# Twelve small layers on one core: later places for four pieces of layer two's keys and values, and a pause of GpSimd in the router

## What is computed

```
x = x + _L0_attn_ref(_layernorm(x), ...)                  # mLSTM and gated MLP
x = x + _L0_ffn_ref(_layernorm(x), wg, shared, experts)   # router, 2 shared and 16 expert blocks
x = x + _L1_xattn_ref(_layernorm(x), ctx_2048, ctx_2048)  # 16 heads, causal, no projections
x = x + _L1_attn_ref(...); x = x + _L1_ffn_ref(...)       # dense attention, quantized linear
x = x + _L2_xattn_ref(_layernorm(x), ctx_2048, mask, wq, bq, wk, bk, wv, bv, wo, bo)  # 16 heads
...
```

## Time and profile before

| | |
|---|---|
| median of three runs | 1213.25 us |
| the profiled execution's own time | 1214.64 us |
| its span, from the first to the last instruction | 1212.8 us |
| TensorE matmuls busy | 1096.0 us, 90% |
| TensorE weight loads busy | 834.8 us, 69% |
| VectorE busy | 655.0 us, 54% |
| ScalarE busy | 548.4 us, 45% |
| GpSimd busy | 223.0 us, 18% |
| the clock that TensorE was granted, mean | 0.954 of full |

### The profile page before, as it was taken

One profiled execution on the slowest core, in us unless ns is written; L12 is line 12 of the kernel. 1 busy time (PEld: TensorE's weight loads), 2 busy tenths in 40 slices (PEclk: granted clock), 3 DMA queues, 4 the chain that ended last, 5 costly groups with the idle time before them and its releaser, 6 DMA issues.

```text
span 1212.8 us, 22806 instructions
## 1 busy us (share of the span) xinstructions
PE 1096.0 (90%) x9168; PEld 834.8 (69%) x9168; DVE 655.0 (54%) x1308; ACT 548.4 (45%) x987; POOL 223.0 (18%) x344
## 2 busy tenths in 40 slices
PE   6888989989999869999787889999999999999885
PEld 2655668865666536777554767788888888887763
DVE  3645252247777267888534644654444445555357
ACT  2132222225666348888553234444444344444365
POOL 4500068002122000000010310011000133222031
PEclk9998999997999889999887899999999999999998
DMA  9611247444663460000200210131111112100000
GB/s 386 264 54 64 82 158 240 156 139 113 181 169 86 162 222 36 2 2 2 113 28 1 87 35 20 35 105 53 36 36 36 52 53 72 60 18 10 1 1 10
DMA packets 38101, 102.46 MB, mean 84 GB/s; under 512 B 4080, under 2 KB 12656, under 8 KB 36336
## 3 DMA queue, kind: packets, MB, share of 16 engines
q1 hardware_dynamic: 33808, 88.91, 22.0%
q0 software_dynamic: 2752, 9.44, 2.5%
q10 hardware_dynamic: 1440, 2.70, 0.6%
HBM read 85.83 MB, written 15.20 MB: 83 GB/s over the span
## 4 chain that ended last, share of the span: by engine, by line
PE 83%; DVE 10%; ACT 3%; issue 2%; DMA 1%; POOL 0%; DVEq 0%; SPq 0%; ACTq 0%; POOLq 0%
PE ps L2161 10%; PE ps L2110 9%; PE ps L433 8%; PE ps L1743 5%; PE ps L1391 5%; PE ps L2144 5%; PE ps L2006 5%; PE ps L2015 4%; PE ps L426 4%; PE ps L488 3%; PE ps L1734 3%; PE ps L1540 3%; PE ps L1076 2%; PE ps L1551 2%; DVE st L1669 2%
## 5 line engine op out<-in xcount | busy, mean ns | idle before, releaser
L2161 PE MATMUL ps<-vv,probT 128*128 128x128 f32 x1024 | 135.3, 275 | 0.2 <-ACT probT L2226 0.2
L2161 PEld LDWEIGHTS ps<-vv,probT 128*128 128x128 f32 x1024 | 124.4, 192 | 0.5 <-ACT probT L2226 0.5
L2226 ACT COPY probT<-ps 128x512 f32<-128x512 f32 (+1 forms) x96 | 45.7, 477 | 121.8 <-PE ps L2144 118.2
L1669 DVE TENSOR_REDUCE st<-ps 128x1 f32<-128x512 f32 x128 | 83.5, 687 | 27.7 <-PE ps L1540 21.5
L2260 ACT ACTIVATE prob<-ps,st,small 128x1024 f32<-128x1024 f32 x64 | 79.9, 1254 | 31.0 <-DVE st L2305 31.0
L2144 PE MATMUL ps<-const,prob 128*128 128x128 f32 x544 | 85.6, 273 | 0.0
L2048 DVE TENSOR_REDUCE small<-vv 128x4 f32<-128x512 f32 x32 | 21.9, 685 | 116.9 <-ACT vv L2031 116.9
L433 PE MATMUL ps<-xT,big 128*128 128x256 f32 x352 | 79.4, 380 | 1.4 <-ACT big L1100 0.7
L1616 ACT ACTIVATE prob<-ps 128x1024 f32<-128x1024 f32 x64 | 65.7, 1029 | 29.0 <-PE ps L1551 27.4
L152 POOL TENSOR_SCALAR small<-small 128x4 f32<-128x4 f32 (+1 forms) x38 | 7.8, 206 | 380.4 <-DVE small L2048 261.1
L2144 PEld LDWEIGHTS ps<-const,prob 128*128 128x128 f32 x544 | 64.2, 141 | 16.7 <-issue 16.4
(11 more groups left out here) (442 smaller groups left out, 2215.5 us busy)
## 6 DMA issues: line engine op xcount, KB each, us to landing
big<-blocks_in SPq DMA_DIRECT2D x22, 768.0 KB, 4.3
big<-ctxT_in SPq DMA_DIRECT2D x32, 512.0 KB, 4.1
key_parts<-w POOLq DMA_DIRECT2D x16, 384.0 KB, 3.4
kt<-key_parts SPq DMA_DIRECT2D x32, 192.0 KB, 3.3
vv<-ctx_in SPq DMA_DIRECT2D x2, 2176.0 KB, 28.7
vv<-early_values SPq DMA_DIRECT2D x4, 1088.0 KB, 12.8
kt<-ctxT_in SPq DMA_DIRECT2D x2, 2048.0 KB, 14.7
kt<-key_parts SPq DMA_DIRECT2D x32, 128.0 KB, 3.1
```

Of the source, the lines that this page charges most:

```text
L1669: dve.tensor_reduce(self.mx[:, u % 2, n:n + 1], k.ps[:, n % 2, :], AX.X, ALU.max).then_inc(s("reduced"), 1)
L2161: last = pe.matmul(k.ps[:, 7, 0:P], k.probT[:, ch * P:ch * P + P], v, start=(ch == 0), stop=(ch == MC))
L2226: copy(k.probT[:, lo:hi], k.ps[:, 5 + t % 2, 0:hi - lo]).then_inc(s(copied), 1)
```

## The change

- `LATE` is 12: pieces 12 to 15 use the second ring, which now lies in `vv` at the columns of batch 1's first half of values. The causal attention reads them, so GpSimd sets the ones column behind that attention's last product (it was done at its start) and counts it on `fsum`; the stores of these pieces wait for it.
- Piece 12 goes from between the router and the experts to behind the causal attention, where 13 was; 13 goes to 14's place, 14 to 15's. Piece 15 goes into the masked attention: its keys behind unit 0's scores, its values behind unit 1's, in banks 4 and 5, and ScalarE copies them ahead of unit 0's exps and ahead of the last queries copy. SyncE stores it, within `reload`.
- GpSimd waits for the fifth `block_h`, the gate of the first expert block, before its last ten split blocks.
- `fsum` is added once piece 15's keys are made (product 31); its readers wait for 2.
- The waits for finished stores at turn 2 on ScalarE and VectorE are taken out.

```diff
-    BANKS = [(4, 5), (0, 1), ... (0, 6), (0, 2), (0, 1), (0, 2), (0, 1), (2, 3)]
-    LATE = 13
+    BANKS = [(4, 5), (0, 1), ... (0, 6), (0, 2), (0, 2), (0, 1), (2, 3), (4, 5)]
+    LATE = 12
...
-        (self.ks, self.vs), (self.late_ks, self.late_vs) = ring(8704), ring(4096)
+        (self.ks, self.vs), (self.late_ks, self.late_vs) = ring(k.big, 8704), ring(k.vv, 2 * MC * VH)
...
     def store(self, queue, n):
+        if n >= self.LATE:
+            queue.wait_ge(self.k.s("fsum"), 1)
...
     def reload(self, sp):
         for b, pieces in enumerate((self.LATE, self.PIECES)):
+            if b:
+                self.store(sp, self.PIECES - 1)
             self.stored(sp, pieces)
...
 # Causal.gpsimd
-        o.step(pool.memset(early.late_vs[:, :, :, 16:17], 1.0))
...
 # Masked.tensor
             if t < 32:
                 scores(t)
+            if t == 0:
+                pe.wait_ge(*self.at("turned_sb", 1))
+                self.early.tensor_keys(pe, 15)
+            if t == 1:
+                pe.wait_ge(*self.at("turned_sb", 2))
+                self.early.tensor_values(pe, 15)
             if t == 2:
-                pe.wait_ge(*self.at("turned_sb", 2))
+                self.early.copied(pe, 15)
                 pe.wait_ge(self.s("queries_dve"), 1)
...
 # Masked.scalar
         queries(1, 2)
+        self.early.scalar_keys(act, 15)
         for t in range(35):
...
-            if t == 2:
-                self.early.stored(act)
...
             if t == 1:
+                self.early.scalar_values(act, 15)
                 queries(3, 3)
...
 # Masked.vector
                 if t == 2:
-                    dve.wait_ge(k.s("fsum"), 1)
+                    dve.wait_ge(k.s("fsum"), 2)
...
-            if t == 2:
-                self.early.stored(dve)
...
 # TensorE in build
             Router.tensor(k, pe, 2)
-            early.tensor(pe, 12)
-            early.copied(pe, 12)
+            early.copied(pe, 11)
             gated.moe_tensor(pe)
             n1.tensor(pe)
+            early.tensor(pe, 12)
+            Norm.tensor(k, pe, 4)
+            early.copied(pe, 12)
+            Dense.tensor(k, pe)
             early.tensor(pe, 13)
-            Norm.tensor(k, pe, 4)
-            early.copied(pe, 13)
-            Dense.tensor(k, pe)
+            Quant.tensor(k, pe, 0)
             early.tensor(pe, 14)
-            Quant.tensor(k, pe, 0)
-            early.tensor(pe, 15)
             Quant.tensor(k, pe, 1)
-            early.copied(pe, 15)
+            early.copied(pe, 14)
             n2.tensor(pe)
...
 # GpSimd in build
             Norm.gpsimd(k, pool, o, 2)
+            pool.wait_ge(s("block_h"), 5)
             split.gpsimd(pool, o, split.BEFORE_MLSTM, len(split.BLOCKS))
-            n1.gpsimd(pool, o, early)
+            n1.gpsimd(pool, o)
+            pool.wait_ge(s("a_product"), 32)
+            pool.memset(early.late_vs[:, :, :, 16:17], 1.0).then_inc(s("fsum"), 1)
...
-            pool.wait_ge(s("early_product"), 2 * early.PIECES)
+            pool.wait_ge(s("early_product"), 2 * early.PIECES - 1)
             pool.tensor_tensor(k.fsum, n1.part, ...).then_inc(s("fsum"), 1)
```

More of the change, by code:

```diff
@@ L1041, with ring @@
     PIECES = 16
-    BANKS = [(4, 5), (0, 1), (2, 0), (7, 6), (0, 6), (7, 0), (0, 6), (7, 0), (0, 6), (1, 2), (0, 6), (0, 2), (0, 1), (0, 2), (0, 1), (2, 3)]
-    LATE = 13
+    BANKS = [(4, 5), (0, 1), (2, 0), (7, 6), (0, 6), (7, 0), (0, 6), (7, 0), (0, 6), (1, 2), (0, 6), (0, 2), (0, 2), (0, 1), (2, 3), (4, 5)]
+    LATE = 12
     def __init__(self, k, keys, values):
         self.k, self.keys_out, self.values_out = k, keys, values
-        def ring(at):
-            return (k.big[:, at:at + 1024].rearrange("p (s m) -> p s m", s=2),
-                    k.big[:, at + 1024:at + 2112].rearrange("p (s g n) -> p s g n", s=2, n=17))
-        (self.ks, self.vs), (self.late_ks, self.late_vs) = ring(8704), ring(4096)
+        def ring(tile, at):
+            return (tile[:, at:at + 1024].rearrange("p (s m) -> p s m", s=2),
+                    tile[:, at + 1024:at + 2112].rearrange("p (s g n) -> p s g n", s=2, n=17))
+        (self.ks, self.vs), (self.late_ks, self.late_vs) = ring(k.big, 8704), ring(k.vv, 2 * MC * VH)
     def made(self, n):
@@ L1067, in tensor @@
     def tensor(self, pe, n):
-        k, (b, pair), (x, y) = self.k, divmod(n, 8), self.BANKS[n]
+        k = self.k
         if n == 0:
@@ L1071, in tensor, with context, tensor_keys, tensor_values @@
         self.free(pe, n)
-        def context(c):
-            return k.kt[:, (b * DC + c) * M:(b * DC + c + 1) * M]
+        self.tensor_keys(pe, n)
+        self.tensor_values(pe, n)
+    def context(self, b, c):
+        return self.k.kt[:, (b * DC + c) * M:(b * DC + c + 1) * M]
+    def tensor_keys(self, pe, n):
+        k, (b, pair), x = self.k, divmod(n, 8), self.BANKS[n][0]
         for c in range(DC):
             for r in range(4):
-                last = pe.matmul(k.ps[32 * r:32 * r + 32, x, :], k.w2("wk", DC)[:, c, 32 * pair:32 * pair + 32], context(c)[:, 512 * r:512 * r + 512],
+                last = pe.matmul(k.ps[32 * r:32 * r + 32, x, :], k.w2("wk", DC)[:, c, 32 * pair:32 * pair + 32], self.context(b, c)[:, 512 * r:512 * r + 512],
                                  start=(c == 0), stop=(c == 1))
         last.then_inc(self.s("product"), 1)
+    def tensor_values(self, pe, n):
+        k, (b, pair), y = self.k, divmod(n, 8), self.BANKS[n][1]
         for t in range(2):
             for c in range(DC):
-                last = pe.matmul(k.ps[:, y, t * D:(t + 1) * D], context(c)[:, (2 * pair + t) * P:(2 * pair + t + 1) * P], k.w2("wv", DC)[:, c],
+                last = pe.matmul(k.ps[:, y, t * D:(t + 1) * D], self.context(b, c)[:, (2 * pair + t) * P:(2 * pair + t + 1) * P], k.w2("wv", DC)[:, c],
                                  start=(c == 0), stop=(c == 1))
@@ L1458, in steps_of_second, with gpsimd @@
             yield lambda: self.spread(pool.tensor_copy, 1, parts, i)
-    def gpsimd(self, pool, o, early):
+    def gpsimd(self, pool, o):
         k, s = self.k, self.s
@@ L2727, in _ @@
             pe.wait_ge(s("xT"), turned_norms(8))
-            pe.wait_ge(s("fsum"), 1)
+            pe.wait_ge(s("fsum"), 2)
             for b in range(B):
@@ L2752, in _ @@
             Router.scalar(k, act)
+            gated.moe_scalar(act)
+            n1.scalar(act)
             early.scalar(act, 12)
             early.store(act, 12)
[L2755 to L2758, removed]
             Norm.scalar(k, act, 4)
@@ L2763, in _ @@
                 Norm.root(k, act, 5, b)
+            early.scalar_keys(act, 13)
+            Quant.root(k, act)
+            early.scalar_values(act, 13)
+            early.store(act, 13)
+            Quant.scalar(k, act, 0)
+            Norm.root(k, act, 6, 0)
             early.scalar_keys(act, 14)
-            Quant.root(k, act)
+            Norm.root(k, act, 6, 1)
             early.scalar_values(act, 14)
             early.store(act, 14)
[L2768 to L2773, removed]
             Norm.table(k, act, ACT.Exp, 1)
```

## The result

The changed kernel takes 1204.6 us in the median of 11 runs (1200.6 to 1208.8), the kernel before 1213.25 us in 11 runs (1209.35 to 1218.55). The ratio is 0.9926, with a 95% interval of 0.9908 to 0.9943: 9.0 us faster by the ratio, 6.9 to 11.2 by its interval. The forecast was 1204.8 us. The profiled execution of the changed kernel took 1206.26 us, with a span of 1204.5 us and a mean granted clock of 0.958 (before: 1212.8 us and 0.954).

The account below looks back on a forecast made before the run. TensorE makes up 83% of the chain, so time comes only where TensorE itself waits or work leaves its path. −7.2 − 0.45 − 0.8 = −8.45 us takes the median 1213.25 to 1204.8 us; own range 1202.5 to 1207.

Parts of the forecast that it names:

- parts 1 and 2: Router: piece 12 leaves and GpSimd waits for the first expert's gate; first `up` starts at 164.5, not 171.71: −7.2 us.
- part 3: Pieces 12, 13, 14 take the places of 13, 14, 15: 0; GpSimd's add leaves VectorE's tensor_scalar before the query matmuls: −0.45 us.
- part 4: Masked attention's opening: piece 15's keys and values hidden in TensorE's waits, clock kept, unit 3's scores earlier: −0.8 us.
- the 1.6 us of clock loss: Router: piece 12's keys took 3.47 us against 1.92 later on; counted within the 6.11 us removed with the piece.
- The clock falling into `up`: Rival at the experts' first `up`: the clock falls anyway and `up` pays 1.6 us, 1206.4 us in all; chance 14%.
- The second rival: Router: the pause frees nothing, `down` waits for the gate, −2.7 us in place of −7.2, 1209.3 us; chance 6%.
- The slower case: Masked units: ScalarE carries the two copies' lag into the rhythm, +15 − 8.45 at 0.5 us a turn, about 1219; chance 4%.
- The signs: Normalizations 0.7 to 0.8 us, router chain 5.4, tensor_scalar 0.17, no clock fall in the opening, unit 3's scores 8.4 us earlier.
- One sign of being wrong: Masked attention's opening: the prediction is wrong if unit 1's scores start more than 2.6 us behind unit 0's.

Follow-up runs that it names:

- e1: Kernel before plus only GpSimd's wait for the first expert's gate, piece 12 still at the router: 1210.85 us, ratio 0.998.
- e5: Kernel before with only piece 15's halves in the masked attention; no pause, place between the two quantized linears empty: 1207.69 us, ratio 0.9941.
- e2: Changed kernel without GpSimd's wait for the first expert's gate: 1208.56 us, ratio 0.9966.
- e3: Changed kernel without piece 15's matmuls and copies in the masked attention, the buffer's old content stored instead: 1207.72 us, ratio 0.9955.
- e6: Changed kernel with piece 12 in the causal attention's opening and no piece between the two quantized linears: 1203.55 us, ratio 0.9922.
- e9: The same program as e6, measured again beside the changed kernel: 1202.27 us, ratio 0.9914.
- e7: Changed kernel with piece 12 in the causal attention's opening and no piece behind the causal attention: 1204.62 us, ratio 0.9921.

## Why the prediction was right, step by step

The large steps, parts 1, 2 and 4, came out by their mechanisms. That the sum came out to 0.3 us is luck: part 3 was wrong by 1.65 us, and the other four rows below, each a little better than forecast, make up for it.

| step | predicted | measured (changed minus before) |
|---|---|---|
| router, parts 1 and 2 | −7.2 | −7.5 |
| first `down` to the dense add | 0 | −0.7 to −1.1 in three traces |
| dense add to queries (part 3) | −0.45 | +1.2 |
| queries to unit 0 | 0 | −0.2 |
| unit 0 to unit 3 (part 4) | −0.8 | −1.2 |
| sum | −8.45 | −8.4 to −8.7 |

**Parts 1 and 2** came out as worked: normalizations in 0.74 us, VectorE's chain 5.6 us for 5.4, the gate ending at 168.10, 0.5 us ahead of `down` at 168.60 (I had 0.9), the end of the split at 217.1 for 219.2. What was wrong inside it is the 1.6 us of clock loss, which I counted as part of piece 12. It belongs to that execution of the kernel before: e1 and e5, piece 12 in its old place, have 5.52 us from the router's matmuls to `up`, not 7.17. The sum was made against that execution, so the loss belonged in it; for the median the step is somewhere between −5.8 and −7.5 us, and no run here tells how often the fall hits piece 12 (one of the three traces that have it there). Without it the touched parts differ by 6.8 to 7.1 us and the medians by 8.65; where the rest of the medians' difference comes from isn't shown.

**The port.** That GpSimd's blocks slow VectorE's two-input operations and not its reduction was read off two rows of before, 1.19 and 0.19 us. e2 settles it. Here the rule that I took from the Trainium skill (SBUF — State Buffer, Who interferes with whom) was enough to know which of the small steps would come free: beside GpSimd's work in e2 the tensor_reduce of L803 keeps its 0.19 us.

**Part 3 failed.** The step "Banks, waits and ScalarE's order at each place are what they were: 0" holds for the order and not for the clock. I took the duration of the keys, 1.92 us, from the piece that stood there before, and never asked what 3.5 us would do, although ScalarE's copy of them stands ahead of the root that VectorE waits for. Read along VectorE's steps behind the dense add, changed against before, it goes so: at the root it falls 1.38 us behind (L190); at L993 it gets 0.46 back, so the −0.45 us was right; and ahead of L1003 it loses 0.30, waiting 1.25 us instead of 0.95. That makes +1.2. In that last wait ScalarE copies the turned input 0.3 us after the turn is done, since its copy of the late values and a table load stand ahead:

```profile
427.17 0.44 PE L227 MATMUL ps<-const,att 128*128 128x128 f32 x2 [1.63 <-DVE att L997]
...
427.96 0.66 ACT L1035 ACTIVATE attT<-ps 128x256 bf16<-128x256 f32 x2
```

So the term that I put at 0 measured +1.7 us, the low clock handed on through ScalarE's queue.

**Part 4** was mis-sized by 0.4 us, for one term. I let the second queries copy and the exps take their turn on ScalarE behind values that end at 454.6, 6.8 us after unit 0's scores began. They end 6.7 us after (444.33), as planned, but each step on ScalarE behind them is a little shorter: the queries copies start 7.23 us after unit 0's scores where I had 7.42, they and the first exp take 1.15 and 1.04 us from start to start instead of 1.24 and 1.1, and the third turn starts 10.07 us after unit 0's scores (447.69), where I had 10.4. The mechanism, clock kept by filled waits, is what e3 shows.

**What I didn't foresee** is 0.7 to 1.1 us between the first `down` and the dense add. Eight traces with the edited rings and a piece behind the causal attention have 243.3 to 245.0 us there, before and e1 244.4 and 244.9, and two traces of one program, e6 and e9, differ by 1.69 us there. So even its existence is doubtful.

**The rivals.** The clock falling into `up` happened in one of the eight traces without piece 12 in the router, e2, where `down` waited for the gate anyway; the seven others, all with the pause, show none. The second rival's size was right for its condition: without what the pause frees I had −2.7 us, and e2, where it is not freed, has −2.61 (both against the trace of before with its fall; −0.95 against e5's router). The slower case didn't occur: units come 4.1 us apart and TensorE is busy 20.00 of 20 us. (Its own terms, 1213.25 + 15 − 8.45, make 1219.8 us where I wrote about 1219.)

**The signs.** The norm, the router chain, L993, the clock through the opening and the experts' `up` are as listed. Unit 3's scores start 11.4 us earlier, of which 2.65 lie ahead of the router and belong to the execution. One sign of being wrong was set wrongly: unit 1's scores start 3.65 us behind unit 0's, over the 2.6 that I named, but 3.64 before as well. The 2.6 fits the wait between the two, which was 2.50 us and is 0.65.

## What to carry to other kernels

Where one stage has two limits a few microseconds apart, on two engines, cost both edits together: here they gave 1.2 and 1.0 us alone and 5.8 as a pair, against a router without a clock fall. When filler work is moved out of a wait that stays, count the clock as well as the work, since the matmuls behind the empty waits of e3 and e7 took 1.6 to 1.8 times as long; and look for an in-order copy that hands a slow TensorE on to the engine that sets the end. Compare kernels by stretches between instructions that both have, and not by the spans of two traces; and when a stretch comes out the same, follow it step by step all the same, since in e5 a gain and a loss of 0.46 us each lay in one.

## What the runs showed of the hardware

The spread of a kernel's own runs, 1196.7 to 1207.0 us of span for the changed kernel, goes mostly with the clock. Over 138 executions of eight kernels, the time at 1.2 GHz (twice the span times what the mean granted clock lacks of 1) explains 72% of the variance within a kernel, and a microsecond more of it makes the span 0.33 us longer. The falls come at different places from execution to execution of the same program: the changed kernel's three traces have them, ahead of a router that all pass at the full clock, at 34.3 and 116.2 us; at 82.9, 100.0 and 117.0 us; and at 34.8, 82.6, 99.7 and 116.7 us.
